# Values by small transfers, one product weight for dt, the skip term inside the projection of x, and new places for the copy of y and the second norm

## The chip, the cores and the metric

The kernel runs on one core of a Trainium2 chip. The metric is the time of one launch on the device in microseconds (us), the median of several runs. The core has five engines that run their own instruction streams and meet through semaphores: PE (TensorE, matmul), DVE (VectorE), ACT (ScalarE), POOL (GpSimd) and SP (SyncE, which here only issues transfers). Matmul results land in PSUM, eight banks of 128 x 512 f32.

## The reference

Eight sequences (batches) of 512 tokens with 128 channels go through a hybrid block: a state-space scan, windowed attention, a short convolution and a small memory attention are computed from the layer-normed input and added, and a second norm and a linear layer follow. What matters here:

```python
xa = layernorm(x)                                  # first norm; then the block's own norm
xn = layernorm(xa) * ln_g + ln_b
xp = xn @ w_xproj                                  # dt_in (64) | B (64) | C (64)
delta = softplus(dt_in @ w_dt + b_dt)
h_t = exp(delta * A) * h_{t-1} + (delta * xn)[:, None] * B_t ;  y_t = h_t @ C_t
ssm_out = (y + xa * D_ssm) @ w_ssm_out
q, k, v = xa @ wq, xa @ wk, xa @ wv                # 16 heads, 4 key/value heads of 8
attn_out = softmax(window scores + bias) @ v_window @ wo   # blocks of 32 tokens, windows of 96
wm = xa @ w_wm + b_wm                              # memory branch
x1 = x + xa + 0.2 attn_out + 0.45 ssm_out + 0.15 conv_out + 0.2 mem_out
out = x1 + layernorm(x1) @ W + bias + lora
```

## The kernel before

Everything is written out by hand: each engine has one function that lists its instructions, and waits on semaphores join them. `run_batches` gives the frame: `front(0)` prepares batch 0, then `body` runs for each of the eight batches, six of them as three turns of a loop of two, and `tail` ends the last. There is a jump after batches 2, 4 and 6.

A body has 64 **slots**, `UNITS`. In slot s, DVE multiplies the input of scan s by B (`unit_input`, L1165) and runs scan s-1 (`unit_scan`, L1177), a recurrence along 512 tokens for two channels times 64 states. ACT makes the decay of unit s+2 (`unit_exp`, L628), PE spreads the input of unit s+2 over the partitions (`unit_u`, L878), and POOL multiplies pairs of scan results by C (`pair_product`, L1364) and every fourth input by B (L1380). PE sums four units' products into y (`reduce_group`, L902, eight records for a group: each f32 matmul shows as two). PE and ACT may go two slots ahead of DVE and no further: they wait for scan s-2. Every fourth unit's input comes by the transfers `uwide` and needs no work of PE.

All other work hangs in tables of slots. `JOB_AT` gives the slot of each single product through the one free bank `jobP`: for the next batch (`p`: the transposes `xaT` and `xnT`, then `dti` and `dtpre`, `B`, `C`, `q`, `k`, `v`), for this batch's memory and convolution (`m`), and for the last batch's end (`t`). A job must wait until the one before it has been copied out of `jobP`. `AT` gives the slots of steps that are not jobs. The attention blocks run at slots 0, 3, 6, 9, 13, 16, 19, ...: scores on PE (L911), two slots later bias and maximum on DVE (L1190; `scores_there` makes DVE wait for the scores ahead of that slot's `unit_input`), exponentials on ACT (L642), and eleven slots later the product with the values `vw` (`values`, L926).

The steps that the change touches:

- **Values.** Job `v` stands in slot 62 of the batch before. PE makes, for each of the 16 blocks, the values of its 96 window tokens (L863: 16 matmuls with 96 columns of x as weight and 32 columns of `wv_s` moving), and ACT copies all to `vw` (L575).
- **dt.** Jobs `dti` (slot 18, L852; ACT copies it out, L562) and `dtpre` (slot 20, L855) give dt_in and dt_in @ w_dt. ACT takes absolute value and Relu (L566, L567), exp (L583, slot 21), DVE adds 1 (`softplus_sum`, L1135, slot 21), ACT takes the logarithm (L588, slot 23, with a table load before and one after), DVE corrects the rounding (L1140, slot 24), POOL does three more steps.
- **Skip term.** `y_start` (L896, slot 5) opens the sum y with diag(D_ssm) times x. `reduce_group` adds the rest. `y_copy` (L634, slot 2 of the next batch) copies the finished y out, and `project` (L957 to L970, slots 0 to 10) sums x, convolution, memory, attention and y by their weights.
- **Second norm.** `root2` on POOL, `normalise2` on ACT (L523, slot 21), then jobs `zT` and `ffn`.

SP's stream has 32 steps of two slots (`m`): each issues two transfers `wide` (L407) for the decays eight slots on, gated by the exponentials; every fourth also two `uwide` (L396), gated by the scans. `load_weights` stands in SP's `front`.

## Time and profile before

| | us |
|---|---|
| median of 3 runs | 1187.52 |
| lowest, highest | 1183.56, 1188.54 |
| profiled execution, its own time | 1187.0 |
| its span, first to last instruction | 1185.2 |
| mean granted TensorE clock | 0.838 of full |
| first scan starts | 45.9 |
| DVE busy | 991.5 |
| POOL busy | 951.2 |
| PE busy | 890.7 |
| ACT busy | 837.1 |

The span is the time from the first to the last instruction of the program; a busy share is the union of an engine's instructions over it. Seven of the eight batches look alike, so one batch (here the stretch from batch 4 to batch 5, which meets at 752 us) stands for all. In a row of the timeline, the bracket at its end is the engine's idle time ahead of it, and what ended that idle time.

### The profile page before, as it was taken

How to read it: one execution, taken by the hardware profiler on the slowest of the kernel's cores; microseconds unless marked ns; L12 is line 12 of the kernel's file. 1: busy time of each engine (PE TensorE's matmuls, PEld its weight loads, DVE VectorE, ACT ScalarE, POOL GpSimd, SP SyncE). 2: the span in 40 equal slices, each digit the busy share in tenths (PEclk: the TensorE clock that was granted, in tenths of full speed). 3: DMA queues.
4: the chain of work that ended last, by engine and by line, in shares of the span. 5: the costliest groups of instructions: out<-in, count | busy, mean ns of one | idle time of the engine just before them, and what ended most of it. 6: DMA issues, size and time to landing. Idle time of an engine off the chain costs nothing. (4 is left out here: it accounts for less than half of the span.)

```text
span 1185.2 us, 19428 instructions
## 1 busy us (share of the span) xinstructions
PE 890.7 (75%) x4372; PEld 370.4 (31%) x4372; DVE 991.5 (84%) x2310; ACT 837.1 (71%) x2247; POOL 951.2 (80%) x667
## 2 busy tenths in 40 slices
PE   4467778687787877878787687877869687787776
PEld 2122334232332324322243223422324232333332
DVE  2598997799887996979969899688997899789992
ACT  4677875777667775687757877577875877657771
POOL 5378996799877996879869899597996799769882
PEclk9667998788797887978779888787898788798888
DMA  4845575566653775555755657464665566567640
GB/s 114 209 113 155 167 191 145 139 161 175 160 143 113 186 175 150 139 134 156 185 143 139 173 150 192 129 153 125 187 171 148 138 166 174 153 160 173 165 117 9
DMA packets 112230, 180.03 MB, mean 152 GB/s; under 512 B 17106, under 2 KB 28902, under 8 KB 112102
## 3 DMA queue, kind: packets, MB, share of 16 engines
q1 hardware_dynamic: 111814, 178.44, 58.1%
q8 instruction: 42, 0.69, 0.3%
q14 instruction: 86, 0.70, 0.2%
q10 hardware_dynamic: 288, 0.20, 0.1%
HBM read 171.18 MB, written 5.05 MB: 149 GB/s over the span
## 5 line engine op out<-in xcount | busy, mean ns | idle before, releaser
L1364 POOL TENSOR_TENSOR prod<-hst,C 128x1024 f32<-128x1024 f32 x256 | 602.5, 2356 | 178.7 <-DVE hst L1177 177.8
L1177 DVE TENSOR_TENSOR_SCAN hst<-decay,bank 128x512 f32<-128x512 f32 x384 | 459.7, 1208 | 23.7 <-POOL prod L1364 20.8
L1165 DVE TENSOR_TENSOR bank<-bank,B 128x512 f32<-128x512 f32 x384 | 262.1, 683 | 87.8 <-PE bank L911 41.8
L628 ACT ACTIVATE decay<-wide,A_rep 128x512 f32<-128x512 f32 x384 | 273.4, 714 | 43.1 <-DVE hst L1177 40.2
L878 PE MATMUL bank<-spread,sel_bc 96*128 96x512 bf16 x384 | 169.2, 442 | 153.4 <-DVE hst L1177 140.3
L642 ACT ACTIVATE prob<-s_sb,nmax 128x96 f32<-128x96 f32 x512 | 184.7, 363 | 0.8 <-DVE nmax L1190 0.3
L902 PE MATMUL bank<-prod,sel_red 128*32 128x512 f32 x1024 | 179.0, 779 | 7.9 <-POOL prod L1364 7.8
L1380 POOL TENSOR_TENSOR uwide<-uwide,B 128x512 f32<-128x512 f32 x128 | 163.0, 1273 | 23.6 <-DMA uwide<-u_rows 23.6
L1177 DVE TENSOR_TENSOR_SCAN hst<-bank,uwide 128x512 f32<-128x512 f32 x128 | 155.1, 1212 | 5.3 <-ACT bank L628 5.3
L911 PE MATMUL bank<-k,q 128*128 128x384 f32 x256 | 130.8, 598 | 12.3 <-DVE nmax L1190 12.0
L878 PEld LDWEIGHTS bank<-spread,sel_bc 96*128 96x128 bf16 x384 | 40.3, 105 | 306.6 <-DVE hst L1177 229.9
L651 ACT ACTIVATE probT<-bank 96x512 f32<-96x512 f32 x128 | 75.3, 588 | 79.0 <-PE bank L918 79.0
L918 PE MATMUL bank<-ident,prob 128*96 128x128 f32 x512 | 90.9, 306 | 26.5 <-ACT ao L658 14.9
L1369 POOL TENSOR_TENSOR prob<-prob,pinv 128x384 f32<-128x384 f32 x128 | 109.2, 853 | 1.4 <-DVE pinv L1198 1.3
L1190 DVE CUSTOM_DVE_ANT_0 s_sb<-bank,bias 128x96 f32<-128x96 f32 x512 | 98.0, 247 | 0.0
L642 ACT ACTIVATION_READ_ACCUMULATOR prob<-s_sb,nmax 128x1 f32 x512 | 96.8, 189 | 0.0
L628 ACT ACTIVATE bank<-wide,A_rep 128x512 f32<-128x512 f32 x128 | 87.2, 681 | 10.1 <-DVE hst L1177 6.7
L918 PEld LDWEIGHTS bank<-ident,prob 128*96 128x96 f32 x512 | 61.3, 139 | 95.9 <-issue 72.5
L911 PEld LDWEIGHTS bank<-k,q 128*128 128x128 f32 x256 | 52.0, 225 | 73.6 <-issue 50.7
L658 ACT ACTIVATE ao<-bank 128x128 f32<-128x128 f32 x128 | 33.9, 265 | 45.4 <-PE bank L926 45.1
L926 PE MATMUL bank<-probT,vw 96*8 96x128 f32 x1024 | 55.4, 291 | 0.2 <-ACT probT L651 0.2
L863 PE MATMUL bank<-wv_s,xaT 128*96 128x32 f32 x256 | 39.4, 332 | 19.8 <-ACT k L542 19.8
(185 smaller groups left out, 1072.5 us busy)
## 6 DMA issues: line engine op xcount, KB each, us to landing
wide<-dt_rows SPq DMA_DIRECT2D x512, 256.0 KB, 4.7
uwide<-u_rows SPq DMA_DIRECT2D x128, 256.0 KB, 4.1
spread<-parts SPq DMA_DIRECT2D x66, 32.0 KB, 3.4
x_sb<-in_L_attn_x_dram SPq DMA_DIRECT2D x8, 256.0 KB, 4.3
dt_rows<-sp_t SPq DMA_DIRECT2D x8, 256.0 KB, 3.9
out_dram<-outb SPq DMA_DIRECT2D x8, 256.0 KB, 4.5
bias<-rel_table SPq DMA_DIRECT2D x12, 48.0 KB, 1.9
u_rows<-uv SPq DMA_DIRECT2D x8, 64.0 KB, 3.6
```

The costliest lines, as they stand in the source:

```text
L628: nc.scalar.activation(to, wide[m % SLOTS][:, s % 2, :], ACT.Exp, scale=A_rep[:, g:g + 1]).then_inc(exp_done, 1)
L642: ins = nc.scalar.activation(prob[:, k % 4, g, :], s_sb[:, k % 2, g, :], ACT.Exp, bias=nmax[:, k % 2, g:g + 1], scale=-1.0, accum_out=psum ...
L878: mm(uP[q][:, :], sel_bc[:, i, :, :].rearrange("k j n -> k (j n)"), spread[p][:, q, :], start=True, stop=True).then_inc(u_ready, 1)
L902: ins = mm(yP[32 * q:32 * q + 32, :], sel_red[:, i, :], prod[:, (i % 2) * 4 + q, :], start=False, stop=(i == GROUPS - 1), skip_group_check ...
L911: mm(sP[:, 0:KVH * 3 * W], q4[:, k, :, :].rearrange("p r q -> p (r q)"), k4[:, :, k * W:k * W + 3 * W], start=True, stop=True).then_inc(s_ ...
L918: ins = nc.tensor.transpose(ptP[0:3 * W, g * 128:(g + 1) * 128], prob[:, k % 4, g, :], ident[:, :])
L1165: v.tensor_tensor(uP[s % 4][:, :], uP[s % 4][:, :], B2[p][:, :], ALU.mult).then_inc(dbx_done, 1)
L1177: v.tensor_tensor_scan(hst[:, s % 4, :], kept, into[:, :], 0.0, ALU.mult, ALU.add).then_inc(scan_done, 1)
L1190: ins = v.tensor_tensor_reduce(s_sb[:, k % 2, g, :], sP[:, g * 3 * W:(g + 1) * 3 * W], bias3[:, row, g, :], 1.0, BIG, ALU.add, ALU.min, nm ...
L1364: g.tensor_tensor(prod[:, 2 * (m % 4):2 * (m % 4) + 2, :], hst[:, 2 * (m % 2):2 * (m % 2) + 2, :], C2[p][:, :].unsqueeze(1).to_broadcast([ ...
L1369: g.tensor_tensor(prob[:, k % 4, :, :], prob[:, k % 4, :, :], pinv[:, k % 4, :].unsqueeze(2).to_broadcast([128, KVH, 3 * W]), ALU.mult) \
L1380: g.tensor_tensor(u, u, B2[p][:, :], ALU.mult).then_inc(gbx_done, 1)
```

## The change

Values: PE makes the values once for each token (4 matmuls of 128 tokens), ACT copies them to a new tile `v_tok`, and twelve transfers of 32 partitions (three or four pieces of 128 bytes on each) spread them to `vw`, three in each of SP's steps 0 to 3 of the batch itself; in batch 0 all twelve follow `load_weights`. PE's `values` waits for the twelve; ACT's job `v` waits for the twelve of the batch before. POOL clears `vw` once.

dt: `w_delta` = w_dti @ w_dt is made once in the beginning (a transpose and a product on PE, two copies on DVE), and job `dtpre` is one product of it with `xnT`. Job `dti` and its copy are gone. The addition of 1 moves from DVE to ACT, right behind the exp.

Skip term: `w_x` takes diag(D_ssm) times `w_ssm` once (one DVE instruction in batch 0's setup); `y_start` is gone, and the first `reduce_group` opens the sum.

Places: the tables move, as the diff shows.

```diff
-PRE = {n: i for i, n in enumerate(["xaT", "xnT", "dti", "dtpre", "B", "C", "q", "k", "v"])}
+PRE = {n: i for i, n in enumerate(["xaT", "xnT", "dtpre", "B", "C", "q", "k", "v"])}
-JOB_AT = {12: ("t", "back"), 14: ("p", "xaT"), 16: ("p", "xnT"), 18: ("p", "dti"), 20: ("p", "dtpre"),
-          22: ("t", "zT"), 25: ("t", "ffn"), 27: ("m", "es0"), 31: ("p", "B"), 32: ("p", "C"), 33: ("m", "pt0"),
-          38: ("m", "conv"), 41: ("m", "es1"), 46: ("m", "es2"), 50: ("m", "pt1"), 51: ("m", "es3"),
+JOB_AT = {13: ("t", "back"), 15: ("p", "xaT"), 17: ("p", "xnT"), 19: ("p", "dtpre"),
+          22: ("t", "zT"), 26: ("t", "ffn"), 28: ("m", "es0"), 32: ("p", "B"), 33: ("p", "C"), 34: ("m", "pt0"),
+          39: ("m", "conv"), 42: ("m", "es1"), 46: ("m", "es2"), 50: ("m", "pt1"), 51: ("m", "es3"),
...
-    "reduce": 3, "y_copy": 2, "project": 0, "proj_copy": 11, "residual": 13, "aggr2": 15, "root2": 16,
-    "normalise2": 21, "ffn": 24, "output": 26,
+    "reduce": 3, "y_copy": 5, "project": 1, "proj_copy": 12, "residual": 14, "aggr2": 16, "root2": 17,
+    "normalise2": 20, "ffn": 25, "output": 27,
-    "ln_stats": 0, "ln_aggr": 2, "ln_root": 4, "ln_apply": 11, "scale_xn": 12, "softplus_exp": 21, "sum": 21,
-    "softplus_logs": 23, "rounding": 24, "log1p": 25, "dt": 26, "u": 27, "high": 30, "r": 32,
+    "ln_stats": 0, "ln_aggr": 2, "ln_root": 4, "ln_apply": 11, "scale_xn": 12, "softplus_exp": 20,
+    "softplus_logs": 21, "rounding": 23, "log1p": 24, "dt": 25, "u": 27, "high": 30, "r": 32,
-    "y_start": 5, "tanh": 38, "gate": 39,
+    "tanh": 39, "gate": 40,
+VALUE_DMA_AT = {0: (0, 1, 2), 1: (3, 4, 5), 2: (6, 7, 8), 3: (9, 10, 11)}
@@ SP, body
+                    if m in VALUE_DMA_AT and not first(B):
+                        window_values(B, VALUE_DMA_AT[m])
@@ SP
+            def window_values(B, which):
+                wait(sp, done["p"], job_count("p", B, "v"))
+                for j, m in (divmod(n, 4) for n in which):
+                    blocks = [n for n in range(NBLK) if 0 <= n - 1 + j < NBLK and (n - 1 + j) % 4 == m]
+                    t0 = (blocks[0] - 1 + j) // 4
+                    sp.dma_start(vw[32 * j:32 * j + 32, blocks[0]:blocks[-1] + 1:4, :, :]
+                                 .rearrange("p n g h -> p n (g h)"),
+                                 v_tok[32 * m:32 * m + 32, t0:t0 + len(blocks), :, :]
+                                 .rearrange("p t g h -> p t (g h)")).then_inc(v_in, 16)
@@ ACT, job v and softplus_exp
-                    ins = nc.scalar.activation(vw[:, :, :, :].rearrange("p n g h -> p (n g h)"), job[0:3 * W, :], ACT.Copy)
+                    wait(act, v_in, B * 16 * N_V_DMA)
+                    ins = nc.scalar.activation(v_tok[:, :, :, :].rearrange("p t g h -> p (t g) h"),
+                                               job[:, 0:128].rearrange("p (a h) -> p a h", h=HD), ACT.Copy)
+                wait(act, sp_step, B * N_SP + SP["exp"])
+                nc.scalar.activation(sp_t[:, :], sp_e[:, :], ACT.Identity, bias=1.0).then_inc(sp_step, 1)
@@ PE, jobs and reduce_group
-                    ins = mm(job[0:DTR, :], w_dti[:, :], xnT[:, :], start=True, stop=True)
-                elif name == "dtpre":
-                    wait(pe, done["p"], job_count("p", B, "dti"))
-                    ins = mm(job[:, :], w_dt_s[:, :], dti[:, :], start=True, stop=True)
+                    ins = mm(job[:, :], w_delta[:, :], xnT[:, :], start=True, stop=True)
-                    for n in range(NBLK):
-                        ins = mm(job[0:3 * W, n * 32:(n + 1) * 32], xaT[p][:, n * W:n * W + 3 * W], wv_s[:, :],
+                    for t in range(NT):
+                        ins = mm(job[:, t * 32:(t + 1) * 32], xaT[p][:, HALO + t * 128:HALO + (t + 1) * 128],
-                mm(yP[:, :], ddiag[:, :], xaT[p][:, HALO:HALO + L], start=True, stop=False,
+                if i == 0:
+                    wait(pe, y_evac, B)
```

**PE where one batch meets the next.** First before, then now, from the values (`wv_s,xaT`) in slot 62 to the second scores (slot 3); `bank<-k,q` are scores, `bank<-spread,sel_bc` the input of a unit, `x4` of `sel_red` a group of y, the rest is `project`.

```order
L863 MATMUL bank<-wv_s,xaT 96x32 x16
L878 MATMUL bank<-spread,sel_bc 128x512
L902 MATMUL bank<-prod,sel_red 32x512 x4
...
L878 MATMUL bank<-spread,sel_bc 128x512
...
L957 MATMUL bank<-xaT,w_x 128x512
...
L911 MATMUL bank<-k,q 128x384
...
L960 MATMUL bank<-cv_v,cs_id 128x512
L961 MATMUL bank<-cs,cs_id 128x512
...
L878 MATMUL bank<-spread,sel_bc 128x512
...
L964 MATMUL bank<-mprobT,dec_m 128x512
```

```order
L883 MATMUL bank<-wv_s,xaT 128x32 x4
L898 MATMUL bank<-spread,sel_bc 128x512
L921 MATMUL bank<-prod,sel_red 32x512 x4
...
L898 MATMUL bank<-spread,sel_bc 128x512
...
L930 MATMUL bank<-k,q 128x384
...
L976 MATMUL bank<-xaT,w_x 128x512
...
L898 MATMUL bank<-spread,sel_bc 128x512
...
L979 MATMUL bank<-cv_v,cs_id 128x512
L980 MATMUL bank<-cs,cs_id 128x512
```

The sixteen narrow products are four, the first scores stand ahead of the first piece of `project`, and of `project` one piece fewer stands ahead of the second scores.

**ACT in slots 19 to 21.** The names: `xn<-bank`, `xa<-bank` are the two reads of `dtpre`, `outb` the second norm, `xn<-xn` the exp of softplus, `sp_t<-xn` the addition of 1, `sp_l<-xn` the logarithm, `decay<-wide` and `bank<-wide` the exponentials that the scans need. First before, then now.

```order
L566 ACTIVATE xn<-bank,cols 128x512
L567 ACTIVATE xa<-bank,cols 128x512
...
L628 ACTIVATE bank<-wide,A_rep 128x512
...
L523 ACTIVATE outb<-x,nbz,rz 128x128 x4
L583 ACTIVATE xn<-xn 128x512
...
L628 ACTIVATE decay<-wide,A_rep 128x512
...
L642 ACTIVATE prob,psum_r<-s_sb,nmax 128x96 x2
L651 ACTIVATE probT<-bank 96x512
```

```order
L584 ACTIVATE xn<-bank,cols 128x512
L585 ACTIVATE xa<-bank,cols 128x512
...
L650 ACTIVATE decay<-wide,A_rep 128x512
...
L543 ACTIVATE outb<-x,nbz,rz 128x128 x4
L664 ACTIVATE prob,psum_r<-s_sb,nmax 128x96 x2
L680 ACTIVATE ao<-bank 128x4x32
L603 ACTIVATE xn<-xn 128x512
...
L605 ACTIVATE sp_t<-xn 128x512
...
L650 ACTIVATE bank<-wide,A_rep 128x512
...
L610 ACT_TABLE_LOAD
L610 ACTIVATE sp_l<-xn 128x512
```

The second norm and the exp stand one slot earlier and ahead of one more decay, the addition of 1 is ACT's, and the logarithm with its table load follows two slots earlier.

**SP in its steps 0 to 4 of a batch, now.** `vw<-v_tok` are the new transfers; before, only the rows `wide` and `uwide` stood there.

```order
L412 DMA wide<-dt_rows 64x2x512 x2
...
L462 DMA vw<-v_tok 32x4x32 x3
...
L412 DMA wide<-dt_rows 64x2x512 x2
L462 DMA vw<-v_tok 32x3x32
L462 DMA vw<-v_tok 32x4x32 x2
...
L412 DMA wide<-dt_rows 64x2x512 x2
L462 DMA vw<-v_tok 32x4x32 x2
L462 DMA vw<-v_tok 32x3x32
...
L412 DMA wide<-dt_rows 64x2x512 x2
L401 DMA uwide<-u_rows 64x2x512 x2
L462 DMA vw<-v_tok 32x4x32 x3
```

The last three stand behind the two `uwide`, which wait for the eighth scan of the batch.

## Rows read from the trace of the kernel before

**Rows 1.** The page's part 1: engine, busy us (share of the span) xinstructions.

```profile
PE 890.7 (75%) x4372; PEld 370.4 (31%) x4372; DVE 991.5 (84%) x2310; ACT 837.1 (71%) x2247; POOL 951.2 (80%) x667
```

**Rows 2.** Groups by line and shape: xcount | busy, mean ns | idle before, releasers.

```profile
L628 ACT ACTIVATE decay<-wide,A_rep 128x512 f32<-128x512 f32 x384 | 273.4, 714 | 43.1 <-DVE hst L1177 40.2 <-ACT mprob L666 1.3 <-DMA wide<-dt_rows 0.4
...
L1165 DVE TENSOR_TENSOR bank<-bank,B 128x512 f32<-128x512 f32 x384 | 262.1, 683 | 87.8 <-PE bank L911 41.8 <-PE bank L878 40.3 <-issue 4.3
...
L863 PE MATMUL bank<-wv_s,xaT 128*96 128x32 f32 x256 | 39.4, 332 | 19.8 <-ACT k L542 19.8
...
L562 ACT ACTIVATE sp_l<-bank 64x512 f32<-64x512 f32 x8 | 4.7, 592 | 8.3 <-PE bank L852 8.3
...
L1135 DVE TENSOR_SCALAR sp_t<-xn 128x512 f32<-128x512 f32 x8 | 3.4, 427 | 31.6 <-ACT xn L583 31.6
```

**Rows 3.** Timeline of DVE, batch 4 to 5: start us, us, what, [idle before].

```profile
747.94 0.70 DVE L1165 TENSOR_TENSOR bank<-bank,B 128x512 f32<-128x512 f32 x1 [2.02 <-issue]
...
751.73 0.70 DVE L1165 TENSOR_TENSOR bank<-bank,B 128x512 f32<-128x512 f32 x1 [2.32 <-PE bank L878]
...
757.53 0.70 DVE L1165 TENSOR_TENSOR bank<-bank,B 128x512 f32<-128x512 f32 x1 [3.98 <-PE bank L911]
...
763.15 0.70 DVE L1165 TENSOR_TENSOR bank<-bank,B 128x512 f32<-128x512 f32 x1
```

**Rows 4.** Timeline of PE in the same stretch.

```profile
745.94 5.33 PE L863 MATMUL bank<-wv_s,xaT 128*96 128x32 f32 x32 [2.85 <-ACT k L542]
...
751.62 1.94 PE L902 MATMUL bank<-prod,sel_red 128*32 128x512 f32 x8
...
754.24 1.91 PE L957 MATMUL bank<-xaT,w_x 128*128 128x512 f32 x2
755.94 1.37 PE L911 MATMUL bank<-k,q 128*128 128x384 f32 x2
...
762.22 0.81 PE L911 MATMUL bank<-k,q 128*128 128x384 f32 x2
```

**Rows 5.** Windows: stretch, us of each engine (x), PEclk, DMA share, GB/s.

```profile
743.40:757.10 13.70, 10.88 (x46) 7.17 (x47) 4.95 (x9) 6.30 (x11) 5.28 (x3) 0.50 0.51 142
757.10:764.00 6.90, 6.90 (x25) 2.71 (x24) 6.46 (x19) 2.61 (x8) 4.37 (x3) 1.00 0.23 75
```

**Rows 6.** Timeline of DVE, slots 21 to 26 of batch 5.

```profile
798.91 0.70 DVE L1165 TENSOR_TENSOR bank<-bank,B 128x512 f32<-128x512 f32 x1 [3.11 <-PE bank L911]
...
804.69 0.43 DVE L1135 TENSOR_SCALAR sp_t<-xn 128x512 f32<-128x512 f32 x1 [3.27 <-ACT xn L583]
...
814.17 1.21 DVE L1177 TENSOR_TENSOR_SCAN hst<-decay,bank 128x512 f32<-128x512 f32 x1
```

**Rows 7.** Timeline of ACT in the same slots.

```profile
802.50 1.63 ACT L523 ACTIVATE outb<-x,nbz,rz 128x128 f32<-128x128 f32 x4
804.04 0.62 ACT L583 ACTIVATE xn<-xn 128x512 f32<-128x512 f32 x1
...
808.34 1.28 ACT L588 ACT_TABLE_LOAD   x1
```

**Rows 8.** Timeline of PE, slots 18 and 19 of batch 5.

```profile
794.01 1.41 PE L852 MATMUL bank<-xnT,w_dti 128*64 128x512 f32 x2
```

**Rows 9.** Timelines of SP and of PE, slots 8 to 11 of batch 5.

```profile
770.30 1.23 SPq L396 DMA_DIRECT2D uwide<-u_rows  x2
...
776.91 0.40 PE L926 MATMUL bank<-probT,vw 96*8 96x128 f32 x8
```

**Rows 10.** Transfers: tiles, issuing queue, xcount, KB each, median us to landing.

```profile
spread<-parts SPq DMA_DIRECT2D x66, 32.0 KB, 3.4
...
wv_s<-in_L_attn_wv_dram SPq DMA_DIRECT2D x1, 16.0 KB, 1.8
```

**Rows 11.** Timelines of SP and of ACT, opening of batch 0.

```profile
49.17 5.71 SPq L407 DMA_DIRECT2D wide<-dt_rows  x8
...
54.44 0.72 ACT L628 ACTIVATE decay<-wide,A_rep 128x512 f32<-128x512 f32 x1 [0.57 <-DVE hst L1177]
```

More of the change, by code:

```diff
@@ L136, in hybrid_block_kernel @@
         w_dti = sb("w_dti", [D, DTR])
+        w_dtiT = sb("w_dtiT", [DTR, D])
+        w_delta = sb("w_delta", [D, D])
         w_B2 = sb("w_B2", [D, 2, NS])
@@ L196, in hybrid_block_kernel @@
         uv = sb("uv", [D, L])
-        dti, dtv, res = sp_l[0:DTR, :], sp_t, sp_r
+        dtv, res = sp_t, sp_r
         parts = sb("parts", [D, 3, L], BF16)
@@ L457, in front @@
                 load_weights()
+                for at in VALUE_DMA_AT.values():
+                    window_values(B, at)
             def store(B, p):
@@ L560, in pre_job @@
                     ins = nc.scalar.activation(xnT[:, :], job[:, :], ACT.Identity, bias=b_col, scale=g_col)
-                elif name == "dti":
-                    ins = nc.scalar.activation(dti[:, :], job[0:DTR, :], ACT.Copy)
                 elif name in "BC":
@@ L793, in _ @@
             pe.wait_ge(w_first, 16 * N_FIRST_DMA)
+            nc.tensor.transpose(bank[0][0:DTR, 0:D], w_dti[:, :], ident[:, :]).then_inc(delta_weight, 1)
             def setup_step(s):
@@ L849, in pre_job @@
                     ins = transposes([xn[:, t, :] for t in range(NT)], 128, 128, job)
-                elif name == "dti":
+                elif name == "dtpre":
                     wait(pe, done["p"], job_count("p", B, "xnT"))
-                    ins = mm(job[0:DTR, :], w_dti[:, :], xnT[:, :], start=True, stop=True)
-                elif name == "dtpre":
-                    wait(pe, done["p"], job_count("p", B, "dti"))
-                    ins = mm(job[:, :], w_dt_s[:, :], dti[:, :], start=True, stop=True)
+                    ins = mm(job[:, :], w_delta[:, :], xnT[:, :], start=True, stop=True)
                 elif name in "BC":
@@ L882, in front @@
                 for name in PRE:
+                    if name == "xnT":
+                        pe.wait_ge(delta_weight, 2)
+                        mm(bank[1][:, 0:D], w_dtiT[:, :], w_dt_s[:, :], start=True, stop=True).then_inc(delta_weight, 1)
+                    if name == "dtpre":
+                        pe.wait_ge(delta_weight, 4)
                     if name == "q":
@@ L889, in front @@
                     unit_u(B, p, s)
-            def y_start(B, p):
-                if first(B):
-                    pe.wait_ge(w_scaled, 1)
-                wait(pe, y_evac, B)
-                mm(yP[:, :], ddiag[:, :], xaT[p][:, HALO:HALO + L], start=True, stop=False,
-                   skip_group_check=True).then_inc(y_started, 1)
             def reduce_group(B, i):
                 wait(pe, prod_done, B * PAIRS + 2 * i + 2)
+                if i == 0:
+                    wait(pe, y_evac, B)
                 for q in range(4):
-                    ins = mm(yP[32 * q:32 * q + 32, :], sel_red[:, i, :], prod[:, (i % 2) * 4 + q, :], start=False,
+                    ins = mm(yP[32 * q:32 * q + 32, :], sel_red[:, i, :], prod[:, (i % 2) * 4 + q, :], start=(i == 0),
                              stop=(i == GROUPS - 1), skip_group_check=True)
@@ L922, in values @@
                 if k == 0:
-                    wait(pe, done["p"], job_count("p", B, "v"))
+                    wait(pe, v_in, (B + 1) * 16 * N_V_DMA)
                 wait(pe, pt_evac, B * NBLK + k + 1)
@@ L1012, in body @@
                             project(B - 1, 1 - p, s - AT["project"])
-                    if s == AT["y_start"]:
-                        y_start(B, p)
                     if s >= AT["reduce"] + 4 and (s - AT["reduce"]) % 4 == 0:
@@ L1070, in skip_diagonal @@
                 v.tensor_scalar(q_mask[:, :], q_mask[:, :], -float(HD) ** -0.5, None, ALU.mult).then_inc(head_tables, 1)
+                dve.wait_ge(delta_weight, 3)
+                v.tensor_scalar(w_delta[:, :], bank[1][:, 0:D], 1.0, None, ALU.mult).then_inc(delta_weight, 1)
             def finish_bias():
@@ L1281, in body @@
                             ln_aggr(B + 1)
-                        if s == AT["sum"]:
-                            softplus_sum(B + 1)
                         if s == AT["rounding"]:
```

30 lines of the change are left out of this document (16 added, 14 removed).

## The prediction

> **What bounds the kernel now.** I read the busy times first. DVE is busy for 84% of the span, POOL 80%, PE 75%, ACT 71% [rows 1]: DVE comes nearest to a bound, and no engine is one all the time. So the question is where DVE stands still. The groups tell it next: ahead of its multiply L1165 it idles 87.8 us in the run, 41.8 for the scores (`bank L911`) and 40.3 for the unit inputs (`bank L878`), both PE's; ahead of the addition of 1, L1135, it idles 31.6 us for ACT's exp in eight instructions [rows 2]. The timelines then give the places, of which there are two in each batch.
>
> The first is where two batches meet. The values begin on PE at 745.94 and hold it for 5.33 us, in 32 records; behind them stand a group of y (1.94), a unit input, the first piece of `project` (1.91) and only then the first scores, which end at 755.94 + 1.37 = 757.31 [rows 4]. DVE idles 2.02 after the jump of the loop, 2.32 for PE's unit input and 3.98 for these scores, and goes on at 757.53 [rows 3]. The next scores end at 762.22 + 0.81 = 763.03 [rows 4], and DVE's multiply in that slot starts at 763.15 [rows 3]: PE sets the time through all of slots 62 to 3.
>
> The second is slots 21 to 24. DVE idles 3.11 us for the scores of slot 19, then 3.27 us for the exp [rows 6], because ACT has the second norm (1.63) ahead of the exp (0.62) [rows 7].
>
> **Values.** 32 records in 5.33 us are 0.167 us each [rows 4]. Eight remain, each with a weight of 128 columns where it was 96; if the weight sets the pace, 0.167 x 128/96 = 0.22, and eight take 1.8 us. PE is free 3.5 us earlier, all of it on the path.
>
> **Order behind the values.** The first scores now stand ahead of the first piece of `project`, 1.91 us at the low clock [rows 4], and one piece fewer stands ahead of the second scores. The first scores thus come 3.5 + 1.9 = 5.4 us earlier. For the second scores the pieces that remain count the same, and the one that falls away is a pair like the first, at the full clock about half of 1.91, 1.0 us: they come 3.5 + 1.0 = 4.5 earlier. That smaller number is the one that lasts, since DVE meets them 0.12 us after they end today. It supposes that the clock rises as long after the values as now: it is 0.50 in the whole stretch from 743.4 to 757.1, and 1.00 from there, with PE busy all of 6.90 us [rows 5]. PE's dense work begins earlier, so I expect the rise to come earlier by about as much. If it came as late as now, PE would do some 3.5 us more of its work at half speed, which doubles 1.8 us: 4.5 becomes 2.7. After the jumps of the loop DVE's own 2.02 us [rows 3] lies partly bare, and ACT and POOL jump too; three of the seven meetings have a jump. I take 4.3 us for each: 7 x 4.3 = **30 us**. Ends: 2 and 5.4 us, so 14 to 38.
>
> **dt and the softplus chain.** Without `dti`, PE has 1.41 us less ahead of slot 19's scores [rows 8], and ACT no copy of 0.59 us (mean) [rows 2]. The transposes of xn move from slot 16 to 17, away from ACT's read in slot 16, so PE reaches the scores some 2.7 us earlier: the wait of 3.11 nearly goes. DVE's wait for the exp goes wholly, with its addition of 0.43 us [rows 6]. But ACT has no less to do: the addition costs it about what the copy did (0.59), and second norm, exp, addition and logarithm with a table load of 1.28 us [rows 7] each way now follow without a pause in slots 20 to 22. Counted from the reads of `dtpre`, ACT does 1.4 (two reads) + 1.6 (norm) + 1.1 (probabilities) + 0.6 + 0.6 + 1.3 + 0.6 + 1.3 + four decays of 0.7 = 11.3 us, while DVE wants five slots of about 1.9. DVE then waits for the probabilities' sums in slot 22 and for the logarithm in slot 23, and the decays of units 24 and 25 come just in time. Going through it slot by slot, scan 20 starts 2.7 us earlier than now, scan 23 hardly 1, and scan 25, at 814.17 now [rows 6], about 3. POOL is left with fewer pauses in which to catch up, so I take 2.7 us for each of batches 1 to 6, and 1.5 for batch 0, whose setup fills the same slots: **18 us**. Ends: nothing (what DVE no longer waits for, it waits for elsewhere) and 5 a batch, so 0 to 33. Batch 7 prepares no next batch and gains nothing here.
>
> **Skip term.** `y_start` leaves PE's slot 5, in which nothing waits for PE: no gain. The copy of y, three slots later, no longer holds ACT while PE finishes y; the decays were early enough anyway. The first group of y waits for that copy, two slots behind it: hidden. The new product in the setup is one DVE instruction, under 1.5 us once at the most, beside the opening's other waits.
>
> **The twelve transfers.** SP issues two `uwide` in 1.23 us, so 0.62 each [rows 9]; twelve are 7.4 us of SP in a batch, in four lots of 1.9. Behind each lot stand two `wide`; they are issued eight slots ahead, and ACT idles for a `wide` only 0.4 us in the whole run before those decays [rows 2]: covered. The last lot is the tight one. It follows the `uwide` pair, so it is issued from 771.5 to 773.4, and PE's product with the values stands at 776.91 [rows 9]. A load of 128 rows of 128 bytes, the same pieces, took 1.8 us (`wv_s`), a `spread` in the traffic of the loop 3.4 [rows 10]. With 1.8 to 3.4 from the last issue at 772.8 it lands between 774.6 and 776.2: 0.7 us or more to spare, cost nothing. In batch 0 the lots stand between `load_weights` and the fifth `wide` pair, issued at 49.17 [rows 11]; its decay on ACT starts at 54.44 [rows 11] with only 0.3 us to spare, so 7.4 us more on SP hold ACT. DVE is busy with setup there for some 2 us, so I take **+5 us**, against **-2 us** for the shorter chain `xnT` to `dtpre` in the opening (1.3 of PE, 0.6 of the copy): +3. Ends: 0 and +8.
>
> On the transfers the Trainium skill, page "DMA: Bandwidth & Descriptors", opening table, says that under 512 bytes a piece falls short of line rate because of a read-modify-write, which speaks against pieces of 128 bytes. Its section "Why small descriptors are slow (HBM only)" excepts transfers within SBUF, as these are. The load with 128-byte rows above, from HBM, was no slower than its neighbours with longer rows, so by row and exception the sum stays; by the rule alone the last lot could come late, the third rival below.
>
> **Sum.** Against the profiled execution's own 1187.0 (span 1185.2; the median of the runs is 1187.52): 1187.0 - 30 - 18 + 3 = **1142 us**.
>
> **Rivals.**
> (a) *The gains are handed on.* Either the clock stays low and the jumps lie bare (2 us a meeting, 14 in all, is gained), or ACT's burst gives the second place nothing. For it: ACT's 11.3 us in five slots, and a clock of 0.50 at just this place [rows 5]. Against it: the waits of 3.98, 3.11 and 3.27 are for work that is truly gone or moved [rows 3, 6]. One of the two gives 1187 - 14 - 18 + 3 = 1158 or 1187 - 30 + 3 = 1160; both, 1176.
> (b) *More than I count.* The meeting gives the full 5.4 and ACT's burst costs little, 4.5 a batch: 1187 - 38 - 29 + 2 = 1122.
> (c) *Slower: the values come late.* PE stands in order, so while it waits in slot 11 the unit inputs behind it wait, and DVE with them. Place: the last lot, in every batch. Up to 776.9 it costs nothing; beyond, every microsecond costs eight. It eats the gain of some 6 us a batch if it lands at 783, that is 11 us after its issue. If the queue held these small pieces for four times a `spread`, 14 us, it would land at 786, 9 us late: 8 x 9 = 72, and 1142 + 72 = 1214. Against it: nothing in the trace of such size takes over 2 us alone; SP's other transfers at that time are only those `uwide` and `wide`. By the rule of the skill alone it would be this case.
> (d) *It does not shorten the path.* The waits shift to POOL, which at 951.2 busy [rows 1] has little room, and the time stays within 0.5%: 1185.
>
> **Chances.** Forecast 0.58, (a) 0.22, (b) 0.09, (c) 0.06, (d) 0.05. About 0.5%, 6 us, is what a measurement can tell from no change. Faster by more: 0.58 + 0.22 + 0.09 = 0.89; the same 0.05; slower 0.06. The range from 1118 to 1172 holds forecast, (b), and (a) but for its case of both.
>
> **What would show it.** PE's values row takes about 1.8 us in place of 5.33, and the first scores end some 5.4 us closer to the last copy of k. DVE's idle time for the scores falls from 41.8 us to under 20, for unit inputs from 40.3 to under 15. The row of the addition is gone from DVE, and a wait for the logarithm, 1 to 3 us a batch, stands ahead of the rounding step. No wait of PE for a transfer to `vw` in slot 11; a wait of ACT for `wide` of about 5 us once, in batch 0. Wrong would be: a low granted clock through slots 0 to 13, where it is high now; waits for POOL of over 3 us a batch; or PE idle for `vw`.

## Result and profile after

The kernel after takes 1174.95 us (median of 4 runs, 1173.91 to 1176.87), the kernel before on the same chip 1188.03 (4 runs, 1183.56 to 1192.24). The ratio is 0.9892, 95% interval 0.9854 to 0.9931. The forecast was 1142, its range 1118 to 1172: the kernel became faster, but by 13 us and not by 45. The profiled execution took 1175.05, its span is 1173.2. Its page, part 1 (compare [rows 1]):

```profile
PE 858.8 (73%) x4151; PEld 356.7 (30%) x4151; DVE 987.2 (84%) x2304; ACT 834.8 (71%) x2247; POOL 951.2 (81%) x668
```

The groups by line (columns as in [rows 2]) tell where DVE and ACT stand idle now:

```profile
L650 ACT ACTIVATE decay<-wide,A_rep 128x512 f32<-128x512 f32 x384 | 273.9, 715 | 83.9 <-DVE hst L1194 62.4 <-DMA wide<-dt_rows 8.4 <-issue 7.3
L1182 DVE TENSOR_TENSOR bank<-bank,B 128x512 f32<-128x512 f32 x384 | 261.5, 681 | 51.4 <-PE bank L930 23.0 <-PE bank L898 18.7 <-issue 4.0
...
L1158 DVE SCALAR_TENSOR_TENSOR sp_t<-sp_t,xn 128x512 f32<-128x512 f32 x8 | 7.4, 928 | 21.8 <-ACT sp_l L610 21.8
...
L1229 DVE SCALAR_TENSOR_TENSOR cs<-bank,cols,cv_a 128x512 f32<-128x512 f32 x8 | 6.0, 751 | 15.3 <-ACT cv_a L714 15.3
...
L1254 DVE TENSOR_TENSOR outb<-bank,x 128x512 f32<-128x512 f32 x8 | 5.5, 692 | 37.7 <-PE bank L994 37.7
```

The waits that the change was forecast to shrink have shrunk: ahead of DVE's multiply 87.8 us became 51.4 and the 31.6 for the exp [rows 2] are gone. Three others have grown. The same groups in the kernel before:

```profile
L1140 DVE SCALAR_TENSOR_TENSOR sp_t<-sp_t,xn 128x512 f32<-128x512 f32 x8 | 6.0, 754 | 5.5 <-ACT sp_l L588 5.5
...
L1212 DVE SCALAR_TENSOR_TENSOR cs<-bank,cols,cv_a 128x512 f32<-128x512 f32 x8 | 6.0, 747 | 5.1 <-ACT cv_a L692 5.1
...
L1237 DVE TENSOR_TENSOR outb<-bank,x 128x512 f32<-128x512 f32 x8 | 5.4, 670 | 9.6 <-PE bank L975 9.6
```

The largest is new: `output`, where DVE adds the linear layer's result to x. Its 9.6 us before were one wait, in `tail`, which is still there; the 28.1 more come from the seven outputs ahead of it, 4.5 to 4.7 us in each of six and 0.4 in the last.

**Where the time went, by slots.** The 512 scans of DVE mark the slots. The difference of their starts, after minus before, summed over the batches (a step that changed its slot is counted where it was; `output`, 1.06 us in each of seven batches, moved from before scan 26 to behind it, so 7.4 us are moved from one row to another):

| stretch | after minus before, us | forecast |
|---|---|---|
| start to first scan | -1.4 | -2 |
| batch 0, slots 5 to 11 | +5.7 | +5 |
| slots 62 to 4, seven meetings | -26.4 | -30 |
| slots 12 to 18 | 0 | 0 |
| slots 19 to 25 | -22.5 | -18 |
| slots 26 and 27 | **+28.7** | 0 |
| slots 28 to 41 | +0.7 | 0 |
| slots 42 to 61 | +3.4 | 0 |
| behind the last scan | 0 | 0 |
| sum (span: -12.0) | -11.8 | -45 |

The forecast's own terms come to -44.6 against -45. What it lacked is the wait in slots 26 and 27. Each row compares one execution with one other, and so carries noise of its own: in skip_alone (below), which gains nothing, the meetings stand at +2.5 and slots 19 to 25 at -3.5.

**The meeting.** DVE, batch 4 to 5 (compare [rows 3]), and PE (compare [rows 4]):

```profile
740.58 0.70 DVE L1182 TENSOR_TENSOR bank<-bank,B 128x512 f32<-128x512 f32 x1 [1.93 <-issue]
...
746.62 0.70 DVE L1182 TENSOR_TENSOR bank<-bank,B 128x512 f32<-128x512 f32 x1 [2.85 <-PE bank L930]
...
754.28 0.70 DVE L1182 TENSOR_TENSOR bank<-bank,B 128x512 f32<-128x512 f32 x1 [2.05 <-PE bank L930]
```

```profile
738.66 1.92 PE L883 MATMUL bank<-wv_s,xaT 128*128 128x32 f32 x8 [2.84 <-ACT k L562]
...
744.49 0.60 PE L898 MATMUL bank<-spread,sel_bc 96*128 96x512 bf16 x1 [1.61 <-DVE hst L1194]
744.88 1.52 PE L930 MATMUL bank<-k,q 128*128 128x384 f32 x2
...
753.34 0.81 PE L930 MATMUL bank<-k,q 128*128 128x384 f32 x2
```

The values take 1.92 us (forecast 1.8). The first scores end 7.7 us behind the start of the values, where it was 11.4 [rows 4]: 3.6 earlier and not 5.4, since PE now stands 1.61 us for a scan that DVE gives late after the loop's jump (1.93, "issue"). The second scores end 15.5 us behind it, where it was 17.1: 1.6 earlier and not 4.5.

The meetings are not alike, and the granted clock sorts them. In all of them it is 0.50 from about the start of the values; the first two rows give how long after that start it goes back to 1.00:

| meeting into batch | 1 | 2 | 3 (jump) | 4 | 5 (jump) | 6 | 7 (loop ends) |
|---|---|---|---|---|---|---|---|
| back at 1.00, before, us | 7.6 | 11.1 | 11.5 | 11.3 | 11.1 | 8.0 | 11.2 |
| back at 1.00, after, us | 7.4 | 5.6 | 11.1 | 5.9 | 11.7 | 6.0 | 4.9 |
| gained, us | 1.2 | 6.9 | 2.4 | 5.2 | 1.6 | 3.5 | 5.7 |

Where the clock came back over 5 us sooner, 5.2 to 6.9 us were gained; where it came back as late as before, 1.2 to 2.4. Windows of after (columns as in [rows 5]), from the meeting into batch 5 and from the one into batch 4, whose values start at 601.17:

```profile
738.70:750.30 11.60, 9.99 (x26) 4.67 (x27) 6.87 (x22) 5.04 (x11) 4.38 (x3) 0.50 0.59 148
607.10:614.00 6.90, 6.90 (x25) 2.75 (x24) 6.60 (x19) 3.94 (x12) 4.50 (x3) 1.00 0.54 144
```

**The new wait.** DVE, then PE, slots 22 to 28 of batch 5:

```profile
795.15 0.79 DVE L1158 SCALAR_TENSOR_TENSOR sp_t<-sp_t,xn 128x512 f32<-128x512 f32 x1 [2.05 <-ACT sp_l L610]
...
800.89 2.32 DVE L1194 TENSOR_TENSOR_SCAN hst<-decay,bank 128x512 f32<-128x512 f32 x2
807.87 0.69 DVE L1254 TENSOR_TENSOR outb<-bank,x 128x512 f32<-128x512 f32 x1 [4.66 <-PE bank L994]
```

```profile
801.07 1.06 PE L937 MATMUL bank<-ident,prob 128*96 128x128 f32 x4 [2.06 <-ACT ao L680]
802.06 2.07 PE L1001 MATMUL bank<-bias_row,ones_row 1*128 1x512 f32 x2
804.05 1.22 PE L994 MATMUL bank<-W,fT 128*128 128x128 f32 x4
805.07 0.63 PE L898 MATMUL bank<-spread,sel_bc 96*128 96x512 bf16 x1
805.50 1.49 PE L930 MATMUL bank<-k,q 128*128 128x384 f32 x2
806.77 1.06 PE L994 MATMUL bank<-W,fT 128*128 128x128 f32 x4
```

DVE has done scan 26 at 803.21 and wants PE's second half of the layer, which ends at 807.83. PE came free of ACT's copy only at 801.07 and then has 6.8 us of queue without a pause. The queue in the kernel before, and DVE's step behind it:

```profile
811.80 1.12 PE L982 MATMUL bank<-bias_row,ones_row 1*128 1x512 f32 x2
812.85 0.71 PE L975 MATMUL bank<-W,fT 128*128 128x128 f32 x4
813.40 0.60 PE L918 MATMUL bank<-ident,prob 128*96 128x128 f32 x4
813.83 0.61 PE L975 MATMUL bank<-W,fT 128*128 128x128 f32 x4
814.28 0.38 PE L878 MATMUL bank<-spread,sel_bc 96*128 96x512 bf16 x1
814.50 0.81 PE L911 MATMUL bank<-k,q 128*128 128x384 f32 x2
```

```profile
815.30 0.67 DVE L1237 TENSOR_TENSOR outb<-bank,x 128x512 f32<-128x512 f32 x1
```

There the layer ended at 814.44, 0.86 us ahead of DVE. Two things differ. The order: a unit input and the scores stood behind the layer, and the shift of the tables put them ahead of its second half, where they take 1.7 us (805.07 to 806.77). And the price: each piece cost little more than half. For that the windows (columns as in [rows 5]) of after, then of before, give the reason:

```profile
798.20:807.90 9.70, 7.45 (x26) 4.02 (x26) 4.92 (x15) 6.55 (x21) 8.69 (x6) 0.50 0.73 204
```

```profile
812.00:820.00 8.00, 6.63 (x41) 3.23 (x40) 7.61 (x25) 6.38 (x18) 7.38 (x5) 1.00 0.94 220
```

The granted clock was 0.50 (1.2 GHz) for the queue now and 1.00 (2.4 GHz) before; so it was, now and before, at the start of the layer in all six batches with a wait of over 4 us. Just ahead of the queue PE now stands 2.01 us for ACT's `probT` and 2.06 for `ao`; the first of the two is this row of PE after:

```profile
798.40 0.61 PE L945 MATMUL bank<-probT,vw 96*8 96x128 f32 x8 [2.01 <-ACT probT L673]
```

The second stands at 801.07 above. That these two stops are what brought the clock down is the likely reading; no run takes them away by themselves.

### The profile page after: what moved, and what is told of

Read it like the earlier page. It is cut to its first block and busy times, and to the rows that moved or that the text cites. A ratio compares the mean times of both kernels' runs of the same rounds, so it can differ in the third digit from the quotient of the medians.

```text
span 1173.2 us, 19130 instructions
## 1 busy us (share of the span) xinstructions
PE 858.8 (73%) x4151; PEld 356.7 (30%) x4151; DVE 987.2 (84%) x2304; ACT 834.8 (71%) x2247; POOL 951.2 (81%) x668
## 5 line engine op out<-in xcount | busy, mean ns | idle before, releaser
L1194 DVE TENSOR_TENSOR_SCAN hst<-decay,bank 128x512 f32<-128x512 f32 x384 | 459.4, 1206 | 15.5 <-POOL prod L1380 14.6
L1182 DVE TENSOR_TENSOR bank<-bank,B 128x512 f32<-128x512 f32 x384 | 261.5, 681 | 51.4 <-PE bank L930 23.0
L921 PE MATMUL bank<-prod,sel_red 128*32 128x512 f32 x1024 | 169.4, 740 | 2.1 <-POOL prod L1380 2.0
L937 PE MATMUL bank<-ident,prob 128*96 128x128 f32 x512 | 98.4, 326 | 49.3 <-ACT ao L680 45.1
L937 PEld LDWEIGHTS bank<-ident,prob 128*96 128x96 f32 x512 | 64.2, 148 | 117.6 <-issue 100.7
L967 PE MATMUL bank<-mdiag,mprob 128*128 128x128 f32 x256 | 43.2, 321 | 9.6 <-ACT mdiag L697 7.7
```

Source lines behind the costliest of these rows:

```text
L921: ins = mm(yP[32 * q:32 * q + 32, :], sel_red[:, i, :], prod[:, (i % 2) * 4 + q, :], start=(i == 0), stop=(i == GROUPS - 1), skip_group_ch ...
L937: ins = nc.tensor.transpose(ptP[0:3 * W, g * 128:(g + 1) * 128], prob[:, k % 4, g, :], ident[:, :])
L1182: v.tensor_tensor(uP[s % 4][:, :], uP[s % 4][:, :], B2[p][:, :], ALU.mult).then_inc(dbx_done, 1)
L1194: v.tensor_tensor_scan(hst[:, s % 4, :], kept, into[:, :], 0.0, ALU.mult, ALU.add).then_inc(scan_done, 1)
```

## Experiments

Each stands against the kernel before on the same chip: 1185.93 us for v_alone, chain_back, ffn_early and lots_in_body; 1185.88 on another chip for sum_dve, conv_back, straight and project_first; 1187.58 for no_bias, sum_alone, skip_alone and all_mended. So what conv_back, straight, project_first and sum_dve differ from ffn_early by is taken across two chips, whose kernels before are 0.05 us apart. "Slots 19 to 25" and "26 and 27" carry the same correction as the table, where `output` stands in its new slot; the recorded expectations count without it (30 for 22.5 us, 36 for 28.7).

**v_alone.** The kernel before with the values by transfers, and nothing else.

```diff
-                    for n in range(NBLK):
-                        ins = mm(job[0:3 * W, n * 32:(n + 1) * 32], xaT[p][:, n * W:n * W + 3 * W], wv_s[:, :],
+                    for t in range(NT):
+                        ins = mm(job[:, t * 32:(t + 1) * 32], xaT[p][:, HALO + t * 128:HALO + (t + 1) * 128],
...
+                    if m in VALUE_DMA_AT and not first(B):
+                        window_values(B, VALUE_DMA_AT[m])
```

> The kernel before with the values by twelve transfers and nothing else of the change. Both theories agree on this part: the meeting of two batches gets shorter by PE's 3.5 us, seven times (25 us), and batch 0 pays about 6 us for the twelve transfers ahead of its fifth pair of wide: 1188 - 25 + 6 = 1169. If the time comes out near 1188, the part that I hold for the gain is not it; if it is below 1160, the rest of the change costs time as a whole.

1171.01 us (1166.47 to 1172.80), ratio 0.9860 (0.9829 to 0.9890). The meetings give 15.0 us, 2.1 each, where the prediction counted 3.5 for the values and 1.0 more for the order; in the kernel after both give 3.8 each. Here too the clock sorts the meetings: into batches 2, 4 and 7 it was back at 1.00 3.4 us sooner than before, and each gained 3.4; into 3 and 5 it was no sooner, and they gained 1.1 and 0.9. In slots 19 to 25 it is 7.2 shorter, 2.3 and 2.5 in two batches and 1.3 and 1.4 in two others. This is not put down to the edit: batch 4 of the kernel before is already 2.4 shorter there than batch 5, and skip_alone moves there by -2.5 to +1.4. So the time fell near the expected 1169 partly by luck. This one part is no slower than the whole change: all other parts together gave nothing that shows.

**chain_back.** The kernel after with the second norm, the exp and the logarithm back in their slots.

```diff
-    "normalise2": 20, "ffn": 25, "output": 27,
+    "normalise2": 21, "ffn": 25, "output": 27,
-    "ln_stats": 0, "ln_aggr": 2, "ln_root": 4, "ln_apply": 11, "scale_xn": 12, "softplus_exp": 20,
-    "softplus_logs": 21, "rounding": 23, "log1p": 24, "dt": 25, "u": 27, "high": 30, "r": 32,
+    "ln_stats": 0, "ln_aggr": 2, "ln_root": 4, "ln_apply": 11, "scale_xn": 12, "softplus_exp": 21,
+    "softplus_logs": 23, "rounding": 24, "log1p": 25, "dt": 26, "u": 27, "high": 30, "r": 32,
```

> The changed kernel with the second norm, the exp, the logarithm, the rounding and POOL's two steps in the slots they had before (21, 21, 23, 24, 25, 26); the addition of 1 stays on ACT. Theory H (handed on): DVE's wait at the output in slot 27 is the old wait of slots 19 to 25 in a new place, since ACT's dense row of work holds PE up and lets its clock fall. Then the wait at the output goes (36 us in slots 26 and 27 in the run) and most of what slots 19 to 25 had gained (30 us) is lost: the time stays within 8 us of the changed kernel's 1175. Theory P (place): the wait comes from the place of the ffn job, one slot ahead of the output, whatever ACT does. Then the wait at the output stays and the old ones come back: 1195 or more.

1171.77 us (1168.94 to 1178.02), ratio 0.9896 (0.9858 to 0.9935), no different from after. Its groups:

```profile
L1158 DVE SCALAR_TENSOR_TENSOR sp_t<-sp_t,xn 128x512 f32<-128x512 f32 x8 | 5.6, 700 | 33.9 <-ACT sp_l L610 33.9
...
L1254 DVE TENSOR_TENSOR outb<-bank,x 128x512 f32<-128x512 f32 x8 | 5.5, 688 | 27.9 <-PE bank L994 27.9
```

Slots 19 to 25 keep 15.4 of the 22.5 us; 12 us more of wait for the logarithm stand against 10 less for the layer. Neither expectation held whole: the wait for the layer stayed but shrank, and the time stayed. What DVE loses in slot 23 it no longer loses in slot 27.

**ffn_early.** The kernel after with the job `ffn` one slot earlier on PE.

```diff
-          22: ("t", "zT"), 26: ("t", "ffn"),
+          22: ("t", "zT"), 25: ("t", "ffn"),
-    "normalise2": 20, "ffn": 25, "output": 27,
+    "normalise2": 20, "ffn": 24, "output": 27,
```

> The changed kernel with PE's two halves of ffn one slot earlier (24 and 25 for 25 and 26); the output stays in slot 27. Theory P: the wait of 4.7 us at the output falls by at least the scores and the unit input that no longer stand ahead of the second half, about 2 to 4 us in each of seven batches: 1146 to 1160. Theory H: PE has the same work at the same low clock, and DVE needs its scores and unit inputs just after; the wait falls by at most 1 us and some of it shows ahead of the multiply: 1168 to 1175.

1149.84 us (1145.51 to 1151.84), ratio 0.9700 (0.9673 to 0.9726).

```profile
L1254 DVE TENSOR_TENSOR outb<-bank,x 128x512 f32<-128x512 f32 x8 | 5.4, 676 | 10.8 <-PE bank L994 10.8
```

Of the 37.7 us, 26.9 are gone, and 25.1 us of the time: two numbers in two tables, moved by one, take most of the new wait away. They change two things at once, however. The scores and the unit input are behind the layer again, and its first half meets a higher clock: 0.71 us here against 1.22 in the kernel after, the granted clock being 1.00 at the start of the layer in five of seven batches. The first and the second half in batch 5's stretch:

```profile
782.77 0.71 PE L994 MATMUL bank<-W,fT 128*128 128x128 f32 x4
...
784.76 1.06 PE L994 MATMUL bank<-W,fT 128*128 128x128 f32 x4
```

**no_bias.** The kernel after without the product of the bias ahead of the layer; its output lacks the bias.

```diff
-                mm(jobP[:, :], ones_row[:, :], bias_row[:, :, :].rearrange("a t d -> a (t d)"), start=True, stop=False,
-                   skip_group_check=True)
                 ffn_half(0)
```

> The changed kernel, but the product that puts the bias into the bank ahead of the linear layer is left out in each batch, so the output lacks the bias. In the trace of the changed kernel this product takes 2.06 us at a granted clock of 0.50 and stands on PE between the transposes of the probabilities and the layer. Theory F (the output step waits for the length of PE's queue, at half clock): DVE's idle time ahead of the output step falls by about 2 us a batch, and the time by 13 to 17 us, to 1158 to 1162. Rival (PE reaches the layer late for another reason, and the product lies beside it): 1170 to 1176.

1159.37 us (1154.04 to 1165.40), ratio 0.9781 (0.9747 to 0.9815).

```profile
L1252 DVE TENSOR_TENSOR outb<-bank,x 128x512 f32<-128x512 f32 x8 | 5.5, 689 | 20.1 <-PE bank L994 20.1
```

The wait fell by 17.6 us, 2.2 in a batch for a product of 2.07. So it is the length of PE's queue, nearly microsecond for microsecond. How much of that length is the low clock is worked out, not shown: the bias and both halves take 2.07 + 1.22 + 1.06 = 4.35 us now and 1.12 + 0.71 + 0.61 = 2.44 before, 1.9 less, and the transposes, the unit input and the scores among them 1.4 less by the rows above. Together that is an estimate of 3.3 us, against a wait of 4.66: most of it, and not all.

**sum_dve** and **sum_alone.** The addition of 1, from both sides: ffn_early with it back on DVE (slot 20), and the kernel before with nothing but it moved to ACT.

```diff
 # sum_dve, against ffn_early
-                nc.scalar.activation(sp_t[:, :], sp_e[:, :], ACT.Identity, bias=1.0).then_inc(sp_step, 1)
+                        if s == 20:
+                            softplus_sum(B + 1)
 # sum_alone, against before
+                nc.scalar.activation(sp_t[:, :], sp_e[:, :], ACT.Identity, bias=1.0).then_inc(sp_step, 1)
-                        if s == AT["sum"]:
-                            softplus_sum(B + 1)
```

> ffn_early with the addition of 1 back on DVE, in slot 20 beside the exp, as it stood beside it in slot 21 before. Theory A (the addition's place is the gain): DVE waits for ACT's exp again, some 3 us and 0.4 of work in each of seven batches, since the exp still stands behind the second norm: slots 19 to 25 lose 15 to 25 us of their 31, about 1169. Theory B (dti's absence is the gain, the two theories differ only here): DVE's wait was for a chain that is now shorter, and slots 19 to 25 lose under 8 us: 1157 or less.

> The kernel before with one edit: the addition of 1 leaves DVE and stands on ACT right behind the exp; all tables as they were. In the kernel ffn_early against sum_dve this place is worth 24.7 us in slots 19 to 25 (-31.1 against -6.4). Theory F (PE's queue on to the output step is what DVE waits for next): slots 19 to 25 lose 18 to 28 us, and slots 26 and 27 take 12 to 25 of it back as a wait of DVE's output step for PE's ffn; in all 1176 to 1184. Rival G (that wait in the changed kernel comes only from the shift of the tables by a slot and from the earlier norm, not from DVE being earlier): slots 26 and 27 stay within 4 us of before, in all 1160 to 1170.

sum_dve: 1175.00 us (1174.05 to 1175.54), ratio 0.9904 (0.9872 to 0.9937). sum_alone: 1186.73 (1184.02 to 1192.01, 10 runs), ratio 0.9997 (0.9978 to 1.0015). The first row is sum_dve's, the second sum_alone's:

```profile
L1155 DVE TENSOR_SCALAR sp_t<-xn 128x512 f32<-128x512 f32 x8 | 3.7, 464 | 41.2 <-ACT xn L603 41.2
```

```profile
L1139 DVE SCALAR_TENSOR_TENSOR sp_t<-sp_t,xn 128x512 f32<-128x512 f32 x8 | 6.4, 796 | 47.7 <-ACT sp_l L590 47.7
```

The whole time of sum_dve is 25 us above ffn_early's. Slots 19 to 25, against before: everything but the addition's move (sum_dve) gives +1.0, since DVE waits 41.2 us for the exp; the addition's move alone (sum_alone) +0.4, since the 31.6 us for the exp went and the wait for the logarithm rose from 5.5 to 47.7; the move with `dti` gone, and the chain in its old slots (chain_back), -15.4; all of it -22.5. Neither shows a gain until the other is there. Both expectations for sum_alone were wrong: DVE never came early enough for the layer to matter, so it says nothing on which of the two was right about the wait there.

**conv_back.** ffn_early with the convolution's job, tanh and gate back in their slots.

```diff
-          39: ("m", "conv")
+          38: ("m", "conv")
-    "tanh": 39, "gate": 40
+    "tanh": 38, "gate": 39
```

> ffn_early with the convolution's job in slot 38, tanh in 38 and gate in 39, as before the change. In slot 39 a group of y and scores stand on PE ahead of the last tap, in slot 38 neither does. If that order makes the 8.5 us that slots 38 to 41 lost, they come back: 1141 to 1143. If the low clock of PE there makes them, nothing moves: 1150.

1139.04 us (1138.05 to 1139.27), ratio 0.9598 (0.9558 to 0.9639).

```profile
L1229 DVE SCALAR_TENSOR_TENSOR cs<-bank,cols,cv_a 128x512 f32<-128x512 f32 x8 | 6.0, 751 | 4.8 <-ACT cv_a L714 4.7
```

The shift by one slot, which the prediction did not price, cost 10.8 us, 8.7 of them in slots 38 to 41 of the profiled executions: in slot 39 of PE a group of y and the scores stand ahead of the last taps, and DVE's gate waits for ACT's tanh behind them. Slots 28 to 41 stand at -1.8 against before in ffn_early and at -9.9 here. Most of these 9.9 come from POOL: in slots 28 to 37 DVE stood 9.4 us for POOL's products in the kernel before and 1.2 here (1.3 in the kernel after). Which part of the change gave them is not shown; neither v_alone nor sum_alone has them in this size (0.0 and -2.0 in slots 28 to 41).

**straight.** ffn_early with the loop of batches 1 to 6 written out.

```diff
-            with eng.Fori(0, (NB - 2) // 2) as k:
+            for k in range((NB - 2) // 2):
```

> ffn_early with the eight batches written out one after another, without the loop. Rival (a) said that the jumps lie bare once PE's values no longer cover them: then the meetings behind a jump (into batches 1, 3, 5 and 7) gain as much as the others, 2 to 3 us each, and the time falls by 5 to 11 us: 1139 to 1145. If the difference between odd and even meetings comes from somewhere else (the clock, a transfer), it stays: 1150. More instructions to fetch could cost a little.

1141.56 us (1139.23 to 1141.94), ratio 0.9623 (0.9583 to 0.9664). Groups of ffn_early, then of straight:

```profile
L1182 DVE TENSOR_TENSOR bank<-bank,B 128x512 f32<-128x512 f32 x384 | 261.9, 682 | 52.2 <-PE bank L930 25.8 <-PE bank L898 20.9 <-DVE cs L1229 2.8
```

```profile
L1182 DVE TENSOR_TENSOR bank<-bank,B 128x512 f32<-128x512 f32 x384 | 261.8, 682 | 42.9 <-PE bank L930 21.7 <-PE bank L898 18.5 <-DVE cs L1229 1.9
```

The meetings ahead of batches 3 and 5, which have a jump, gain 7.16 and 5.94 us on the kernel before instead of 3.04 and 2.56; the one ahead of batch 7, where the loop ends, gains 5.7 instead of 7.0. So leaving a jump out is worth 3.4 to 4.1 us, more than DVE's own pause of about 2: without it the clock is also back at 1.00 sooner, 4.1 and 4.9 us behind the start of the values in these two meetings against 10.8 and 9.9 in ffn_early. The meeting ahead of batch 4, which has no jump, gains 2.3 more as well, so a part of this is spread. The Trainium skill, page "Runtime: NRT & Kernel Launch", section "Instruction fetch mechanics", says that a taken branch outside the fetched window stalls the fetch, and that full unrolling is therefore preferred; the 8.3 us agree with it.

**project_first.** ffn_early with the first piece of `project` ahead of the scores again.

```diff
-    "project": 1,
+    "project": 0,
```

> ffn_early with project back in slots 0 to 10, so that its first piece stands ahead of the first scores again. By the prediction's step the first scores come 1.9 us and the second 1.0 us later at each meeting: 7 to 13 us slower, 1157 to 1163. v_alone, which kept that order, gained only 15 of the 25 us that I gave it at the meetings. If instead the shorter values are all that counts, nothing moves: 1150.

1153.71 us (1150.39 to 1157.66), ratio 0.9720 (0.9670 to 0.9771). The medians are 3.9 us apart from ffn_early and the times overlap; in the profiled executions the meetings gain 20.0 us instead of 28.7. By these the order is worth up to 9 us and may be worth nothing that shows; the 7 to 13 expected is not confirmed.

**skip_alone.** The kernel before with the skip term folded into `w_x`.

```diff
-                    if s == AT["y_start"]:
-                        y_start(B, p)
+                    v.scalar_tensor_tensor(w_x[:, :], w_ssm[:, :], dssm_col, w_x[:, :], ALU.mult, ALU.add).then_inc(w_scaled, 1)
```

> The kernel before with the skip term alone moved: y_start and its diagonal are gone, the diagonal goes into w_x once, the first group opens y; the copy of y stays in slot 2. The prediction's price was zero: 1183 to 1189. Rival: the product of slot 5 stands at the low clock between PE's scores and the next unit inputs and is worth 1 to 2 us a batch: 1170 to 1180.

1188.07 us (1181.22 to 1192.49, 10 runs), ratio 1.0008 (0.9978 to 1.0039): nothing, as forecast.

**lots_in_body.** The kernel after with batch 0's twelve transfers in SP's steps 0 to 3, as in the other batches.

```diff
-                    if m in VALUE_DMA_AT and not first(B):
+                    if m in VALUE_DMA_AT:
-                for at in VALUE_DMA_AT.values():
-                    window_values(B, at)
```

> The changed kernel with batch 0's twelve transfers in SP's steps 0 to 3 of its body, as in all other batches, in place of behind load_weights. If they cost batch 0 its 5.9 us by holding back the fifth pair of wide, slots 5 to 11 of batch 0 get back to 22.7 us from 28.6 and the time falls by 4 to 6: 1170. If the 5.9 us come from the longer opening work (the added copies and the clearing of vw), nothing moves: 1175.

1171.11 us (1169.51 to 1171.95), ratio 0.9876 (0.9852 to 0.9899). In the kernel after SP's queue and ACT read, in the opening:

```profile
47.14 8.26 SPq L462 DMA_DIRECT2D vw<-v_tok  x12
55.44 5.19 SPq L412 DMA_DIRECT2D wide<-dt_rows  x8
```

```profile
60.49 0.72 ACT L650 ACTIVATE decay<-wide,A_rep 128x512 f32<-128x512 f32 x1 [8.07 <-DMA wide<-dt_rows]
```

Twelve issues cost 0.69 us each, and ACT waits 8.07 us once. With them in the body, batch 0's slots 5 to 11 are back within 0.8 us of before.

**all_mended.** ffn_early, conv_back, lots_in_body and straight in one.

> The changed kernel with all that the other runs showed put together: ffn one slot earlier on PE, the convolution's job, tanh and gate back in slots 38 and 39, batch 0's twelve transfers in SP's steps 0 to 3 as in the other batches, and the loop written out. If the four savings lie in different places and add up: 1149.8 (ffn_early) - 10.8 (conv_back against it) - 8.3 (straight against it) - 4.5 (batch 0, from lots_in_body) = 1126, give or take 4. If they share a cover (one engine that is next, POOL above all), 1132 to 1139.

1128.74 us (1124.75 to 1131.50), ratio 0.9495 (0.9465 to 0.9525). The savings add up within the 4 us allowed (1126 expected), as they should where they lie at four places. DVE's waits in it (who, for what: us, times, longest):

```profile
DVE bank L1180 <- PE bank L896: 26.7, 15, 11.1
DVE bank L1180 <- PE bank L928: 22.3, 21, 1.9
DVE sp_t L1156 <- ACT sp_l L608: 22.1, 8, 8.4
DVE hst L1192 <- POOL prod L1378: 14.2, 16, 1.6
```

## Why the prediction was wrong

- **The meeting, -30:** held in size (-26.4), partly by luck. The values' 1.8 us was 1.92. That the clock would rise earlier by about as much did not hold at the two meetings whose jump is taken: into batch 5 it is back at 1.00 11.7 us behind the start of the values, and was 11.1 behind it before, so PE does the work that moved up at half speed. The prediction had priced that case at 2.7 us; it measured 1.6 and 2.4. Into batches 2, 4 and 7 the clock came back 5.4 to 6.3 us sooner, and they gained 5.2 to 6.9, more than 4.5. The uniform 4.3 is near the mean of two different cases, 3.8.
- **dt and softplus, -18:** held (-22.5), and its sign for the wait that follows too: 2.05 us for the logarithm, within the 1 to 3 forecast. sum_alone and sum_dve show that it needs the addition's move and the rest together; the working had added both without saying that neither pays by itself.
- **Opening, +3:** +4.3. One wait of ACT for `wide` of 8.07 us instead of 5, of which 5.7 came through.
- **Skip term, 0, and the steady transfers, 0:** both held. PE hardly waited for `vw`, 0.9 us once, as its weight loads show in the kernel after:

```profile
L945 PEld LDWEIGHTS bank<-probT,vw 96*8 96x8 f32 x1024 | 17.5, 89 | 80.5 <-issue 54.1 <-ACT probT L673 25.4 <-DMA vw<-v_tok 0.9
```

```profile
vw<-v_tok SPq DMA_DIRECT2D x80, 16.0 KB, 3.1
```

  They landed in 3.1 us, inside the bounds of 1.8 and 3.4 [rows 10]. By the rule under 512 bytes alone it would have been rival (c); the exception for transfers within SBUF, in the Trainium skill, page "DMA: Bandwidth & Descriptors", section "Why small descriptors are slow (HBM only)", decided rightly.
- **The step that failed** is the one behind "Going through it slot by slot": it ended at scan 25 and let the 2.7 us a batch run on to the end. It named what is late next on ACT (probabilities, logarithm, decays), and not what is late next on PE. The next thing that DVE takes from PE there is the layer, for `output`, with 0.86 us to spare in the kernel before; the prediction has no term for it, so it stood at nothing. The change also took `output` one slot on and the layer with it, behind a unit input and the scores, so the move gave no room, and PE's queue there fell to half clock. It measured 28.7 us: the whole miss but 4. ffn_early (26.9 us of wait and 25.1 of time gone) and no_bias (17.6 and 15.6) show that PE's queue ahead of the layer is what DVE waits for; how the 28.7 divide between the order and the clock stays open.
- **Not priced:** the shift of the convolution by a slot. In the sum it hid behind gains in slots 28 to 37, most of them the 8 us less that DVE waits for POOL there; conv_back shows 10.8 us.
- **The rival nearest to the result** was (a) with both cases, 1176. The size is right, and "the gains are handed on" too, but mostly for another cause. Its first condition, a clock that stays low and a jump that lies bare, came true at two meetings of seven; ACT's burst handed back a part (the wait for the logarithm rose by 16.3 us) and not the gain. The rest was handed on at the layer, which (a) does not name.

## What to carry to other kernels

When a stall is taken from one engine, walk on along every engine that feeds it, to the next two or three things that it takes from each, and write down how much each has to spare now: where nothing else changes, the engine can draw ahead of the other only by what that one has to spare. Here the step with under 1 us to spare in the trace of before was the next wait. And price a step that "only" moves by one slot by what stands ahead of it in its new place; try the pieces of a change apart and together: here the addition's move showed no gain alone, nor the rest of its chain without it, and with both that stretch gained 22 us; one job in the wrong slot took it all.
